# A gated cross-attention kernel with routed experts: attention values for two groups of heads at a time, score maxima moved within the slices, and their rows sent ahead of the second norm

## The chip, the core and the metric

The kernel runs on one core of a Trainium2 chip. The metric is device time in microseconds (us), the median of several runs. The core has five engines that run their own instruction streams and meet only at semaphores: TensorE (PE, matrix products into the accumulator memory PSUM; its weight loads are listed as PEld), VectorE (DVE), ScalarE (ACT), GpSimd (POOL) and SyncE (SP, which here only issues DMAs). Each engine takes its instructions in the order in which the program wrote them.

## What is computed

For 32 sequences of 112 tokens (width 256) and contexts of 375 rows, the reference computes a gated cross-attention with 16 heads of 16 columns, and then a gated mixture of 8 experts, 2 for each token:

```
x = x + tanh(g_xattn) * attention(layernorm(x), ctx, ctx)        # Q, K, V with bias, softmax, Wo, bo
s = softmax(layernorm(x) @ w_router.T);  w, e = top_k(s, 2)
x = x + tanh(g_ffn) * sum_k w_k * expert_{e_k}(layernorm(x))     # silu(t w1) * (t w3), times w2
```

All of it is in float32. The inputs are drawn so that the projections' biases and the router's weights matter.

## The kernel before

The program has two parts. The first, up to 636 us in the trace, is attention with the router, one sequence after the other. The second works through 63 tiles of 128 routed tokens, and the change doesn't touch it.

**The attention loop** is a software pipeline written by hand: on every engine a function `step(i)` runs for i from -3 to 32, and within a step most engines go through 12 slices, k = 0 to 11. Step i works on five sequences at once: the attention proper of b = i, the score maxima of c = i+1, the value projection of s = i+2, norm, query and key projection of a = i+3, and the output projection of e = i-1. The second norm and the router's logits are those of r = i-2. Once in four steps, from i = 6 on, the router's choice for a unit of four sequences is worked out on DVE, in six parts: `route(u, 0..3)` in a step that I call a **routed step** (i = 6, 10, 14, ...), at k = 2, 5, 8 and 11, and `route(u, 4)` and `route(u, 5)` in the step behind it, a **settled step** (i = 7, 11, ...), at k = 2 and 5. The other two of every four are **plain steps**. A short set of statistics for the first norm (L706 and L709, and in the settled ones L556) runs at k = 8 of the routed and the settled steps.

**The pieces on PE**, with their lines:
- `exps(b, k)`, L816: two products with 224 columns in every slice. They recompute the scores of a pair of heads, already less the maxima, and ACT turns them into `probs` (L466). The maxima come in as one more row of `stack`, row 96, for each half of the heads; so k = 0 waits for the rows of the first half and k = 6 for those of the second (`s_nmrow`).
- `maxes(c, t)`, L839: two products with 376 columns, t = 0 to 7, into one pair of PSUM banks. DVE reduces them (L692), and PE may not write the next pair before DVE is done (`s_max`). They stand in slices 0, 1, 3, 4, 6, 7, 9 and 10, directly behind `exps` or `values`.
- `values(b, g)`, L830: 12 products that use 32 columns of the array each, four side by side, for one of four groups of heads. (The trace has two records for each.) They stand one group at a time, in slices 4, 7 and 10, and the fourth in slice 1 of the next step. `probs` has two buffers.
- `key_proj` (L850), `value_proj` (L845), the query projection (L947), the output projection (L986), turns of blocks (L855 for the negated maxima, L921, L859, L967, L939) and the logits (L865).

**The way of the maxima's rows**: DVE reduces (L692), PE turns the 112 x 8 block (L855: half 1 in slice 1, half 0 in slice 5), ACT copies it out (`negmax_out`, L518: half 1 in slice 3, half 0 in slice 6), POOL sends it by two DMAs into row 96 of `stack` (`nm_rows`, L304), and `exps` of slice 6 or of the next step's slice 0 waits until they have landed. POOL runs one list for each step: the second norm of r (L322), `nm_rows` of half 1, the bias for x (L329), a scatter of slots (L310), `nm_rows` of half 0, the four products and the difference that make the split query (L345, L346, L349), and a second scatter.

**Low parts of the keys**: ACT writes the high part of a key block (L492, slices 4 and 9) and DVE the low part (L683, slices 5 and 10), both out of PSUM. Two later pieces of PE reuse these banks and wait for DVE's L683: `value_proj` in slice 6, and the logits in slice 11:

```
if k == 6 and s is not None:
    if a is not None:
        pe.wait_ge(s_klo, DC * a + 1)
    ...
    value_proj(s, 1, BC)
```

In slice 4 DVE takes, ahead of its reduction, a reciprocal and the scaling of the attention output (L670, L673), and in slice 10 the residual of x (L678) ahead of L683.

## Time and profile before

| | us |
|---|---|
| median of 3 runs | 960.62 (959.65 to 963.28) |
| the profiled execution | 959.3 |
| its span, from the first to the last instruction | 957.6 |
| PE busy in the span | 858.1 (90%) |
| DVE, ACT, POOL busy | 492.6, 417.8, 475.0 |
| attention loop from the exps of step 4 to those of step 28 | 446.19 for 24 steps, 18.59 each |

PE's busy time counts overlapping matrix products once, from the start of a group to its modelled end, and the end of one group lies a little behind the start of the next. So the length of a piece in the middle of a stream is read from the chain of waits, where pieces stand end to end, and not from the timeline. TensorE's granted clock is 1.00, its full 2.4 GHz, in all the windows of steps that are spoken of below.

### The profile page before, as it was taken

The page shows a single profiled execution, that of the slowest core. Times are in us where ns is not written, and L with a number is a line of the kernel's source. Part 1 is how long each engine was busy: PE and PEld are TensorE (multiplying, and loading weights), DVE is VectorE, ACT ScalarE, POOL GpSimd, SP SyncE. Part 2 cuts the span into 40 slices and gives each one's busy share as a digit, 9 for nine tenths or more (in the row PEclk, how much of TensorE's full clock was granted, in tenths as well). Part 3 has the DMA queues.
Part 4 walks back from the last instruction along what each step waited for, and adds up shares of the span by engine and source line. Part 5 has one row for each costly group of instructions (what it writes and reads, how often), then busy time and mean ns, then how long its engine had stood idle before and what let it go on. Part 6 is the DMA issues. An engine that isn't in the chain of part 4 may idle for free.

```text
span 957.6 us, 20971 instructions
## 1 busy us (share of the span) xinstructions
PE 858.1 (90%) x7152; PEld 679.4 (71%) x7152; DVE 492.6 (51%) x1155; ACT 417.8 (44%) x1083; POOL 475.0 (50%) x565
## 2 busy tenths in 40 slices
PE   1689999999999999999999999871699999999995
PEld 1467778777878877787778777660477777777774
DVE  1266666765775875775786676646122222222221
ACT  1245555655555565555556555440222222222221
POOL 0654443345455445545544554444366566666553
PEclk9899999999999999999999999995799999999998
DMA  6555665667677666557656654308243443443442
GB/s 174 132 134 138 140 164 137 162 149 179 146 157 163 157 148 154 128 137 163 137 111 141 141 129 112 76 26 191 45 61 62 67 62 62 67 62 62 67 61 27
DMA packets 99246, 110.87 MB, mean 116 GB/s; under 512 B 28668, under 2 KB 80628, under 8 KB 99144
## 3 DMA queue, kind: packets, MB, share of 16 engines
q1 hardware_dynamic: 78936, 91.41, 41.4%
q0 software_dynamic: 18240, 16.83, 11.2%
q10 hardware_dynamic: 1968, 1.31, 0.5%
q8 instruction: 60, 0.98, 0.5%
q14 instruction: 42, 0.34, 0.1%
HBM read 34.11 MB, written 16.15 MB: 52 GB/s over the span
## 4 chain that ended last, share of the span: by engine, by line
PE 76%; DMA 11%; issue 4%; DVE 3%; POOL 3%; SPq 1%; ACTq 1%; ACT 0%; POOLq 0%; DVEq 0%
PE ps L1038 15%; PE ps L839 10%; PE ps L816 9%; PE ps L845 8%; PE ps L1073 8%; PE ps L850 8%; DMA stack<-negmax_t 7%; PE ps L830 7%; PE ps L986 3%; PE ps L1055 2%; DVE negmax L692 2%; POOL stack L304 2%; PE ps L1061 1%; PE ps L939 1%; DMA out_dram<-y,idx 1%
## 5 line engine op out<-in xcount | busy, mean ns | idle before, releaser
L692 DVE TENSOR_REDUCE negmax<-ps 112x2 f32<-112x750 f32 x256 | 240.6, 940 | 179.8 <-PE ps L839 178.3
L466 ACT ACTIVATE probs<-ps 125x448 f32<-125x448 f32 x384 | 208.6, 544 | 246.0 <-PE ps L816 243.5
L816 PE MATMUL ps<-stack 97*125 97x224 f32 x768 | 191.6, 333 | 19.4 <-DMA stack<-negmax_t 19.3
L816 PEld LDWEIGHTS ps<-stack 97*125 97x125 f32 x768 | 129.5, 188 | 47.0 <-DMA stack<-negmax_t 25.6
L839 PE MATMUL ps<-stack 96*112 96x376 f32 x512 | 143.6, 362 | 13.1 <-DVE negmax L692 7.1
L402 POOL DMA_INDIRECT out_dram<-y,idx x63 | 99.9, 1585 | 98.6 <-issue 56.7
L795 DVE TENSOR_TENSOR h<-silu,ps 128x352 f32<-128x352 f32 x63 | 32.8, 521 | 170.9 <-PE ps L1038 170.9
L304 POOL DMA_DIRECT2D stack<-negmax_t x128 | 70.9, 559 | 94.1 <-ACT negmax_t L518 79.4
L322 POOL TENSOR_SCALAR xn<-xa,mv,rstd 112x256 f32<-112x256 f32 x31 | 38.1, 1229 | 159.2 <-DVE rstd L570 159.2
L536 ACT ACTIVATE silu<-ps 128x352 f32<-128x352 f32 x63 | 29.2, 464 | 193.2 <-PE ps L1038 193.2
L845 PE MATMUL ps<-wv_sb,ctx_t 128*125 128x256 f32 x384 | 99.9, 382 | 1.4 <-DVE bo_gated L731 0.9
L830 PE MATMUL ps<-probs,v_sb 125*32 125x112 f32 x3072 | 100.1, 263 | 0.2 <-ACT probs L466 0.2
L839 PEld LDWEIGHTS ps<-stack 96*112 96x112 f32 x512 | 71.8, 177 | 38.2 <-issue 16.6
L310 POOL DMA_INDIRECT slot_table<-pay,slots_i x64 | 62.6, 978 | 67.6 <-PE ps L830 55.7
L850 PE MATMUL ps<-ctx_t,wk_sb 128*128 128x375 f32 x256 | 93.5, 488 | 0.7 <-ACT q_raw L499 0.7
L1073 PE MATMUL ps<-w_sb,h_t 128*128 x378 | 92.1, 380 | 0.7 <-ACT h_t L540 0.7
L1038 PE MATMUL ps<-w_sb,xg_t 128*128 x252 | 86.2, 464 | 0.6 <-ACT xg_t L544 0.6
L1073 PEld LDWEIGHTS ps<-w_sb,h_t 128*128 128x128 f32 x378 | 72.0, 191 | 20.4 <-issue 0.9
L830 PEld LDWEIGHTS ps<-probs,v_sb 125*32 125x32 f32 x3072 | 69.3, 109 | 14.8 <-ACT probs L466 0.3
L393 POOL DMA_INDIRECT xg<-xn_scratch,idx x63 | 61.6, 977 | 29.2 <-issue 18.9
L845 PEld LDWEIGHTS ps<-wv_sb,ctx_t 128*125 128x125 f32 x384 | 68.8, 188 | 8.1 <-issue 1.3
L1038 PEld LDWEIGHTS ps<-w_sb,xg_t 128*128 128x128 f32 x252 | 48.1, 191 | 18.6 <-issue 1.9
(163 smaller groups left out, 1198.5 us busy)
## 6 DMA issues: line engine op xcount, KB each, us to landing
stack<-split SPq DMA_DIRECT2D x256, 150.0 KB
stack<-split SPq DMA_DIRECT2D x128, 94.0 KB
ctx_t<-in_ctx_dram SPq DMA_DIRECT2D x32, 375.0 KB, 4.9
stack<-split SPq DMA_DIRECT2D x128, 56.0 KB
out_dram<-xa SPq DMA_DIRECT2D x32, 112.0 KB, 4.4
xn_scratch<-xn SPq DMA_DIRECT2D x32, 112.0 KB, 4.1
w_sb<-in_L_ffn_w_dram SPq DMA_DIRECT2D x8, 352.0 KB, 4.2
xa<-in_x_dram SPq DMA_DIRECT2D x6, 448.0 KB, 5.9
```

The source lines that it names most:

```text
L304: gp.dma_start(dst[:, :, SKP + SQ * h:SKP + SQ * h + SQ], negmax_t[4 * h:4 * h + 4, half, :].bitcast(f32)).then_inc(s_nmrow[half][c % NSLO ...
L310: gp.indirect_dma_start(table, bass.IndirectOffsetOnAxis(ap=slots_i[:, u % 2, GB * k + j:GB * k + j + 1], axis=0), pay[:, UNITS[u][j], k, ...
L402: gp.indirect_dma_start(out, bass.IndirectOffsetOnAxis(ap=idx[:, t % NI, 0:1], axis=0), y[:, t % NY, :], None, compute_op=ALU.add).then_in ...
L466: act.activation(probs[:, g % 2, ch, :], ps[0:KW, EXPB + k % 2, 0:4 * SQ], ACT.Exp).then_inc(s_exp, 1)
L692: dve.tensor_reduce(negmax[:, half, :, p4], ps[0:SQ, MAXB:MAXB + 2, 0:SK], axis=AX.X, op=ALU.max, negate=True).then_inc(s_max, 1)
L816: last = pe.matmul(ps[0:KW, EXPB + k % 2, QW * m:QW * m + QW], stack[:, b % NSLOT, p, KW * ch:KW * ch + KW], stack[:, b % NSLOT, p, SKP:KQ ...
L830: last = pe.matmul(ps[32 * j:32 * j + 32, PVB, SQ * g:SQ * g + SQ], v_sb[:, b % NSLOT, ch, head, :], probs[:, g % 2, ch, SQ * j:SQ * j + S ...
L839: last = pe.matmul(ps[0:SQ, MAXB + h, 0:SKP], stack[0:ONE_ROW, c % NSLOT, t, SKP + SQ * h:SKP + SQ * h + SQ], stack[0:ONE_ROW, c % NSLOT, ...
L845: last = pe.matmul(ps[0:KW, bank, 0:EMB], ctx_t[:, s % NSLOT, n, KW * ch:KW * ch + KW], wv_sb[:, n, :], start=(n == 0), stop=(n == DC - 1))
L850: last = pe.matmul(ps[:, bank, 0:SK], wk_sb[:, n, P * m:P * m + P], ctx_t[:, a % NSLOT, n, :], start=(n == 0), stop=(n == DC - 1))
L1038: last = pe.matmul(ps[:, bank, 0:F], xg_t[:, t % NS, k, :], w[k][:, bass.ds(e, 1), :].rearrange("p e f -> p (e f)"), start=(k == 0), stop= ...
L1073: last = pe.matmul(ps[:, YB, 0:EMB], h_t[0:n, c, :], w2_sb[0:n, c, bass.ds(e_o, 1), :].rearrange("p e d -> p (e d)"), start=(c == 0), stop ...
```

## The change

Four things are written differently:
- **Values in pairs.** `values(b, 0)` and `values(b, 1)` stand together in slice 7, `values(b, 2)` and `values(b, 3)` together in slice 1 of the next step. For this `probs` gets a third buffer (three scratch tiles of the second part move in memory to make room), and the waits for free buffers and POOL's waits for `s_pv` ahead of its scatters follow.
- **Maxima.** A table `MAX_AT` puts the eight `maxes` into slices 0, 1, 2, 4, 6, 7, 8 and 10, on PE as the last piece of the slice but for those of slice 11, on DVE at the same slices.
- **Rows of the maxima.** ACT's `negmax_out` of half 1 moves from slice 3 to slice 2, ahead of the copy of `pv_t` (L478); POOL's `nm_rows` of half 1 goes in front of the second norm (L322).
- **Half 0.** Its turn on PE moves from slice 5 to slice 6, behind `exps`, and ACT's copy behind `q_raw` (L499).

The core of the diff:

```
+    NPR = 3
-        probs = sb("probs", [KW, 2, KC, 4 * SQ])
+        probs = sb("probs", [KW, NPR, KC, 4 * SQ])
+        MAX_AT = (0, 1, 2, 4, 6, 7, 8, 10)
 # gpsimd
+                if b is not None:
+                    nm_rows(b, 1)
                 if r is not None:
...
-                if b is not None:
-                    nm_rows(b, 1)
...
-                    gp.wait_ge(s_pv, 4 * b + 1)
+                    gp.wait_ge(s_pv, 4 * b)
...
-                    gp.wait_ge(s_pv, 4 * b + 3)
+                    gp.wait_ge(s_pv, 4 * b + 2)
 # scalar
-                            wait(act, s_pv, 4 * b + g - 1)
+                            wait(act, s_pv, 4 * b + g - NPR + 1)
...
+                    if k == 2 and b is not None:
+                        ...
+                        negmax_out(b, 1, BB_)
                     if k == 2 and e is not None:
...
-                    if k == 3 and b is not None:
...
-                        negmax_out(b, 1, BB_)
...
-                    if k == 6 and c is not None:
-                        negmax_out(c, 0, BA)
                     if k == 6 and a is not None:
...
+                    if k == 6 and c is not None:
+                        negmax_out(c, 0, BA)
 # vector
-                    if k % 3 != 2 and c is not None:
-                        t = k // 3 * 2 + k % 3
+                    if k in MAX_AT and c is not None:
+                        t = MAX_AT.index(k)
 # tensor
                     if k == 1 and e is not None:
+                        values(e, 2)
                         values(e, 3)
-                    if k % 3 == 1 and k > 1 and b is not None:
-                        values(b, k // 3 - 1)
-                    if k % 3 != 2 and c is not None:
-                        maxes(c, k // 3 * 2 + k % 3)
+                    if k == 7 and b is not None:
+                        values(b, 0)
+                        values(b, 1)
...
-                    if k == 5 and c is not None:
+                    if k == 6 and c is not None:
...
                         negmax_turn(c, 0, BA)
...
+                    if k in MAX_AT and c is not None:
+                        maxes(c, MAX_AT.index(k))
```

**PE, slices 2 to 6** of one step, before (from `exps` of slice 3, behind the key projection of slice 2). L816 is `exps`, L839 `maxes`, L939 the turn of `pv_t`, L830 `values`, L947 the query projection, L855 the turn of the maxima, L845 a value projection:

```order
L816 MATMUL ps<-stack 125x224 x2
L839 MATMUL ps<-stack 112x376 x2
L939 MATMUL ps<-ident,pv_t 112x128 x4
L816 MATMUL ps<-stack 125x224 x2
L830 MATMUL ps<-probs,v_sb 32x112 x12
L839 MATMUL ps<-stack 112x376 x2
L816 MATMUL ps<-stack 125x224 x2
L947 MATMUL ps<-xn_t,wq_sb 128x112 x4
L855 MATMUL ps<-ident,negmax 8x112
L816 MATMUL ps<-stack 125x224 x2
L839 MATMUL ps<-stack 112x376 x2
L845 MATMUL ps<-wv_sb,ctx_t 125x256 x2
```

The same place now, from the key projection (L852) on. All lines stand two further down up to here: L818 is `exps`, L841 `maxes`, L941, L949, L857 and L847 are the others:

```order
L852 MATMUL ps<-ctx_t,wk_sb 128x375 x2
L841 MATMUL ps<-stack 112x376 x2
L818 MATMUL ps<-stack 125x224 x2
L941 MATMUL ps<-ident,pv_t 112x128 x4
L818 MATMUL ps<-stack 125x224 x2
L841 MATMUL ps<-stack 112x376 x2
L818 MATMUL ps<-stack 125x224 x2
L949 MATMUL ps<-xn_t,wq_sb 128x112 x4
L818 MATMUL ps<-stack 125x224 x2
L857 MATMUL ps<-ident,negmax 8x112
L847 MATMUL ps<-wv_sb,ctx_t 125x256 x2
L841 MATMUL ps<-stack 112x376 x2
```

The group of values has left the place between the two `maxes`, the first `maxes` stands a slice earlier, the turn of the maxima stands behind `exps` of slice 6, and the value projection ahead of the `maxes`.

**DVE, slices 2 to 5 of a routed step**, before: L588 to L593 are `route(u, 0)`, L692 the reduction of the maxima, L670 and L673 the scaling of the output, L683 the low part of the keys:

```order
L588 TENSOR_REDUCE r_max<-lg 112x4
L589 TENSOR_TENSOR r_eq<-lg,r_max 112x32
L590 TENSOR_TENSOR r_eq<-r_eq,first_e 112x32
L591 TENSOR_REDUCE r_col<-r_eq 112x4
L592 TENSOR_TENSOR r_mask<-r_eq,r_col 112x32
L593 SCALAR_TENSOR_TENSOR r_lg<-r_mask,lg 112x32
L692 TENSOR_REDUCE negmax<-ps 112x2
L670 RECIPROCAL rsum<-ps 112x16
L673 TENSOR_TENSOR o_nat<-ps,rsum 112x256
L692 TENSOR_REDUCE negmax<-ps 112x2
L683 SCALAR_TENSOR_TENSOR split<-ps,bk_sb,split 128x375
```

Now (L694 is the reduction, L685 the low part):

```order
L694 TENSOR_REDUCE negmax<-ps 112x2
L590 TENSOR_REDUCE r_max<-lg 112x4
L591 TENSOR_TENSOR r_eq<-lg,r_max 112x32
L592 TENSOR_TENSOR r_eq<-r_eq,first_e 112x32
L593 TENSOR_REDUCE r_col<-r_eq 112x4
L594 TENSOR_TENSOR r_mask<-r_eq,r_col 112x32
L595 SCALAR_TENSOR_TENSOR r_lg<-r_mask,lg 112x32
L672 RECIPROCAL rsum<-ps 112x16
L675 TENSOR_TENSOR o_nat<-ps,rsum 112x256
L694 TENSOR_REDUCE negmax<-ps 112x2
L685 SCALAR_TENSOR_TENSOR split<-ps,bk_sb,split 128x375
```

The reduction of t = 2 stands ahead of the router's part, and the router's part directly ahead of the scaling. In a settled step `route(u, 4)` stands in the same place.

**DVE, slices 7 to 10 of a settled step**, before: L706, L709 and L556 are the statistics, L678 is the residual:

```order
L692 TENSOR_REDUCE negmax<-ps 112x2 x2
L706 BN_STATS st<-xa 112x6 x2
L709 BN_AGGR mv<-st 112x2 x2
L556 TENSOR_SCALAR half<-mv 112x4
L692 TENSOR_REDUCE negmax<-ps 112x2
L678 SCALAR_TENSOR_TENSOR xa<-ps,tanh_g,xa 112x256
L683 SCALAR_TENSOR_TENSOR split<-ps,bk_sb,split 128x375
```

Now:

```order
L694 TENSOR_REDUCE negmax<-ps 112x2 x3
L708 BN_STATS st<-xa 112x6 x2
L711 BN_AGGR mv<-st 112x2 x2
L558 TENSOR_SCALAR half<-mv 112x4
L680 SCALAR_TENSOR_TENSOR xa<-ps,tanh_g,xa 112x256
L685 SCALAR_TENSOR_TENSOR split<-ps,bk_sb,split 128x375
```

The third reduction has moved ahead of the statistics, which now stand directly ahead of the residual and the low part.

## Rows read from the trace of the kernel before

**Rows 1.** Windows: length, busy time by engine, clock, DMA share; 24 steps, then steps 16 to 19.

```profile
129.34:575.53 446.19, 431.80 (x4462) 354.56 (x4462) 309.57 (x718) 256.13 (x666) 217.97 (x304) 1.00 0.65 147
351.77:370.05 18.28, 17.89 (x187) 14.69 (x186) 11.45 (x25) 10.84 (x29) 9.42 (x14) 1.00 0.67 162
370.05:388.66 18.61, 17.87 (x187) 14.67 (x186) 11.04 (x22) 10.58 (x27) 9.44 (x14) 1.00 0.60 134
388.66:407.76 19.10, 18.36 (x194) 15.10 (x194) 15.35 (x44) 10.70 (x28) 9.60 (x14) 1.00 0.60 132
407.76:425.88 18.12, 17.86 (x187) 14.66 (x186) 13.54 (x34) 10.58 (x27) 9.28 (x13) 1.00 0.58 137
```

**Rows 2.** Waits in the same 24 steps: total us, times, longest.

```profile
PE ps L816 <- DMA stack<-negmax_t: 12.8, 24, 1.1
```

**Rows 3.** Chain of waits in step 19, end to end: start, us, piece.

```profile
409.63 0.71 PE ps L830 x24
410.35 0.53 PE ps L839 x2
...
411.39 1.27 PE ps L850 x4
...
412.88 0.35 PE ps L839 x2
413.23 0.44 PE ps L939 x4
...
416.74 0.48 PE ps L816 x2
```

**Rows 4.** Timeline of PE: start, length, line; prologue, step 19, step 30.

```profile
32.37 1.13 PE L845 MATMUL ps<-wv_sb,ctx_t 128*125 128x256 f32 x4 [0.43 <-DVE split L683]
...
415.17 1.05 PE L947 MATMUL ps<-xn_t,wq_sb 128*128 128x112 f32 x8
416.24 0.26 PE L855 MATMUL ps<-ident,negmax 112*8 112x112 f32 x1
...
615.15 0.60 PE L839 MATMUL ps<-stack 96*112 96x376 f32 x2 [0.49 <-DVE negmax L692]
...
627.68 0.78 PE L830 MATMUL ps<-probs,v_sb 125*32 125x112 f32 x24
628.39 0.26 PE L855 MATMUL ps<-ident,negmax 112*8 112x112 f32 x1
```

**Rows 5.** Timeline of ACT in step 19, slices 2 and 3.

```profile
411.43 0.54 ACT L466 ACTIVATE probs<-ps 125x448 f32<-125x448 f32 x1 [0.57 <-PE ps L816]
...
413.35 0.24 ACT L518 ACTIVATE negmax_t<-ps 8x112 fp32r<-8x112 f32 x1
```

**Rows 6.** Timeline of DVE: routed step 18, settled step 19, and step 30.

```profile
393.12 0.18 DVE L588 TENSOR_REDUCE r_max<-lg 112x4 f32<-112x32 f32 x1
...
394.46 0.94 DVE L692 TENSOR_REDUCE negmax<-ps 112x2 f32<-112x750 f32 x1
...
402.18 0.74 DVE L706 BATCH_NORM_STATS2 st<-xa 112x6 f32<-112x256 f32 x2
...
403.12 0.16 DVE L604 TENSOR_TENSOR r_exp<-lg,r_max 112x32 f32<-112x32 f32 x1
...
403.50 0.93 DVE L612 TENSOR_TENSOR cum<-cum,r_new 112x8 bf16<-112x8 bf16 x1
...
412.22 0.18 DVE L622 TENSOR_REDUCE r_inv<-r_exp 112x4 f32<-112x32 f32 x1
...
413.43 0.94 DVE L692 TENSOR_REDUCE negmax<-ps 112x2 f32<-112x750 f32 x1
414.28 0.25 DVE L670 RECIPROCAL rsum<-ps 112x16 f32<-112x16 f32 x1
414.56 0.42 DVE L673 TENSOR_TENSOR o_nat<-ps,rsum 112x256 f32<-112x256 f32 x1
...
416.01 0.60 DVE L683 SCALAR_TENSOR_TENSOR split<-ps,bk_sb,split 128x375 fp32r<-128x375 f32 x1
```

**Rows 7.** Issue to landing of the maxima's row DMAs, 200 to 580 us.

```profile
DMA to landing us min/median/max: 1.8/4.3/5.6
```

**Rows 8.** Timeline of POOL in routed step 18: the second norm, the last product of the query.

```profile
393.45 1.24 POOL L322 TENSOR_SCALAR xn<-xa,mv,rstd 112x256 f32<-112x256 f32 x1 [4.64 <-DVE rstd L570]
...
403.28 1.14 POOL L349 TENSOR_TENSOR split<-q_msk,split 128x448 fp32r<-128x448 f32 x1
```

More of the change, by code:

```diff
@@ L111, in flamingo @@
         idx = sb("idx", [P, NI, 2], i32)
+        e_cmp, e_mul, e_mul2 = (sb(n, [1, TW, NE]) for n in ("e_cmp", "e_mul", "e_mul2"))
         xg, xg_t = sb("xg", [P, NXG, EMB]), sb("xg_t", [P, NS, DC, P])
```

9 lines of the change are left out of this document (4 added, 5 removed).

## The prediction

> **What bounds the kernel now.** I read the windows of the attention loop first. In 24 steps PE is busy 431.8 of 446.2 us, DVE 309.6, ACT 256.1 and POOL 218.0 [rows 1]. So PE's list sets the pace, 18.59 us a step, and the other engines count only where PE waits for them. The table of waits names one place with a wait in every one of the 24 steps: `exps` of slice 6, for the rows of the maxima of half 1, 12.8 us in all, 0.53 a step and 1.1 at most [rows 2]. The change can gain in two ways: by a shorter list on PE, and by taking this wait away. I then put together the new order from the lengths in the chain and looked for what is late next.
>
> I count from **T, the end of `exps` in slice 2**. End to end, undisturbed pieces take: key projection 1.27, `maxes` 0.35, turn of `pv_t` 0.44 [rows 3], `exps` 0.22 (224 columns where `maxes` has 376; between 409.42 and 409.63 of the chain, estimated from 0.35 x 224/376), query projection 0.88 (1.05 less an overlap of 0.17) [rows 4], value projection 0.87 (the 1.13 of a lone one less 0.26, by which such a piece overlaps the one before).
>
> **The shorter list.** One group of values takes 0.71, the `maxes` behind it 0.53 instead of 0.35 [rows 3]. So leaving the 32-column pieces costs 0.18. Entering costs some 0.14: the 24 records stand for six rounds of 112 columns x four side by side, 0.095 each by the tempo of the other pieces, 0.57 in all, and 0.71 less that is 0.14. That is an estimate; its bounds are 0 and 0.2. Four groups apart have four entries and four exits, two pairs have two of each: 2 x 0.14 + 2 x 0.18 = 0.64 saved. In slice 1 the piece behind the values is now the small turn L855, which in step 30 ends 0.19 behind them (628.65 against 628.46) where 0.10 is its own length [rows 4]: 0.09 more. **0.73 a step.** That the `maxes` stand behind a large piece I cost at nothing: 0.35 behind `exps` is 2 x 376 columns at 2.4 GHz plus 0.03, so there is nothing left to hide. (Below nothing isn't excluded: 0.03 x 4.)
>
> **The wait for the rows.** Step 19 takes 18.12 [rows 1]. In it `exps` of slice 6 ends 0.72 behind the end of L855 (417.22 against 416.50) where 0.22 would do, and L855 ends 0.28 behind the query projection, since it waits for DVE, where 0.10 would do [rows 3, 4]. So a step without waits is 18.12 - 0.50 - 0.18 = 17.44, and in the new order 17.44 - 0.73 = **16.71**.
> The rows need 3.15 us from the end of L518 to the start of `exps` in step 19 (413.59 to 416.74) [rows 3, 5], with an idle time of 0.24; with the mean idle of 0.53 that is 3.44, with the longest 4.0. Now L518 stands in slice 2, behind its exponential, which starts at T + 0.04; the next ACT instruction starts 0.44 later [rows 5], so L518 ends at T + 0.72. POOL is free then: the norm L322 (1.24) [rows 8], which ended 0.2 behind L518 before, inside the 0.63 from L518 to POOL's DMA, now comes after and is wanted only in slice 9. Rows land so that `exps` starts at T + 4.16 (3.87 to 4.7) and ends at T + 4.64.
>
> **What is late next: DVE.** Only `exps` and the turn of `pv_t` are left between `maxes` 2 and 3, and they share PSUM banks.
> - PE ends `maxes` 2 at T + 1.62. DVE reduces from 1.65 to 2.59 (0.94) [rows 6]. PE starts `maxes` 3 at 2.65, and alone it takes 0.60 [rows 4]: 3.25, where 2.85 would be undisturbed.
> - DVE reduces t = 3 from 3.28; L683 starts 0.86 behind that, at 4.14, and takes 0.60 [rows 6]: 4.74. The value projection of slice 6 waits for it: start 4.80, and 1.13 for a lone one [rows 4] is T + 5.93.
> - Undisturbed it would end at 1.62 + 0.22 + 0.44 + 0.22 + 0.35 + 0.22 + 0.88 + 0.22 + 0.10 + 0.87 = 5.14; with the rows alone at 4.64 + 0.97 = 5.61.
> So a **plain step** waits 0.79, of which the rows add 0.03 in their latest cases: 16.71 + 0.82 = 17.53, against 18.28 and 18.61 before.
>
> **Routed and settled steps.** Before, the router's part ran on DVE in the shadow of the key projection, ahead of t = 2. Now it runs between t = 2 and the scaling. It takes 1.34 in a routed step (393.12 to 394.46) and 1.21 in a settled one (412.22 to 413.43) [rows 6].
> - Routed: free at 1.65 + 0.86 = 2.51, router's part to 3.85, L670 and L673 another 0.28 + 0.37 to 4.50, t = 3, L683 from 5.36 to 5.96, value projection from 6.02 to 7.15: it waits 2.01.
> - Settled: the same with 1.21: 7.02, 1.88.
> In slices 8 to 10 it is alike. From the end E of the value projection of slice 6, PE ends `maxes` 6 at E + 4.40 (`maxes` 0.35, `exps` 0.22, two groups 1.29, turn 0.35, `maxes` 0.35, `exps` 0.22, key projection 1.27, `maxes` 0.35). DVE is free at 5.29, then come the statistics (0.94) and in the routed step four short instructions (0.38 and a last one of 0.15) [rows 6], or one more in the settled step (0.22), then L678 (0.39) and L683 (0.60): ready at 7.81 or 7.50. The logits would start at E + 7.16 (another 0.22 + 0.19 + 0.87 + 0.22 + 0.35 + 0.22 + 0.87, less the overlap of two pieces, 0.16 to 0.18). With 0.08 for a lone start they wait 0.7 or 0.4. Plain steps have nothing there.
> Routed: 16.71 + 2.01 + 0.7 + 0.48 for the ranks (PE busy 18.36 against 17.88) [rows 1] = **19.90**, against 19.10 before. Settled: 16.71 + 1.88 + 0.4 = **18.99**, against 18.12 in step 19.
>
> **The sum.** Four steps: 17.53 + 17.58 (one of the plain ones has three more short DVE instructions) + 19.90 + 18.99 = 74.0, against 4 x 18.59 = 74.36: -0.36, and for the 24 steps -2.2. Steps 1 to 3 and 28 have no router's part: 4 x -0.9 = -3.6. In the last steps no projections stand between the `maxes`, and PE would wait for DVE there (615.15, 0.60 after 0.49 idle [rows 4], is this case); the last two groups of values end 0.58 later than one did: +1, bounds -1 and +4. Together **-4.8**: 959.3 becomes 954.5. The median of the runs lies 1.3 above the profiled execution, so 955.8; I say **956**. The second part isn't touched.
>
> **Rivals.**
> - *The router's work stays hidden* (936). If DVE had slack that I don't see, so that routed and settled steps waited like plain ones, four steps would be 70.6, -3.7, and the 24 steps -22. Against it: DVE takes its list in order, and 1.65 + 0.94 is fixed by PE's `maxes` 2. Chance 0.13.
> - *The rows land late* (970, slower). They are now sent 1.5 us earlier, deeper in SP's 16 copies into `stack`. From DMA issue to landing they take 1.8 to 5.6, median 4.3, over both halves [rows 7]; half 1 in step 19 took about 2.5 of the 3.15. Above 3.76 from L518 each 0.1 costs 0.1 in the 16 steps without router's part, and up to the 4.9 or so at which it shows in the others too. At 4.65 that is 0.9 x 16 = +14. It decides from 4.4 on (+10, above the time before). Chance 0.14.
> - *DVE and POOL block each other* (961). L612 took 0.93 [rows 6], and it ends where POOL's L349 ends, at 404.42 [rows 8], while its like take 0.15 to 0.2. The norm L322 now runs from T + 2.5 to T + 3.7, beside the router's part. Had that to wait, it would cost 0.8 in six steps, +5. Against it: in step 18 the six instructions ran beside L322 (393.45 to 394.69) [rows 8] and took no more than 1.34. Chance 0.05. The Trainium skill ("SBUF — State Buffer", Who interferes with whom) says that a DVE instruction with two SBUF inputs contends with a GpSimd instruction that reads SBUF, and that the one issued second fully blocks. By that rule the time would be this rival's; the trace agrees at L612 and does not at L322.
> - *The pairs don't shorten the list* (965). If an entry costs nothing and the group's length is its own, 0.28 x 31 = 9 of the gain is missing. Chance 0.05, inside "same".
>
> **Chances.** My sum 0.63, with a range of its own of 950 to 962, since 0.1 a step is 3 us. About 0.5% (4.8 us) is what a measurement of this kernel can tell from no change: below 955.8 is faster, above 965.4 slower. Faster 0.30 + 0.13 = 0.43, same 0.33 + 0.05 + 0.05 = 0.43, slower 0.14. The range 941 to 966 leaves out most of the first two rivals.
>
> **What would show it.** In the profile after: the wait of PE for the row DMAs gone or under 0.2 a step; in its place waits of L841 (`maxes` 3) and of L847 for DVE, L847's 0.4 to 0.8 in plain steps and nearly 2 in routed ones; `values` as 48 records in about 1.29; steps of 17.5, 17.6, 19.9 and 19.0. It is wrong if routed steps are shorter than 19, if L818 still waits over half a microsecond for its rows, or if the pairs take over 1.4.

## The result and the profile after

| | before | changed |
|---|---|---|
| median of 4 runs each | 961.24 us (959.65 to 963.28) | 1007.0 us (998.6 to 1012.07) |
| profiled execution, span | 959.3, 957.6 | 1012.07, 1010.3 |
| granted clock of TensorE, mean over the span | 0.971 | 0.930 |

The ratio is 1.0466 (95% interval 1.0378 to 1.0555): slower by 45.8 us, where I had forecast 956 and a range of 941 to 966.

Windows of the changed kernel: first the stretch of time of [rows 1], then the same 24 steps (4 to 27), then steps 16 to 19. Columns as in [rows 1].

```profile
129.34:575.53 446.19, 412.46 (x4076) 344.60 (x4076) 281.15 (x649) 229.02 (x609) 197.95 (x278) 0.94 0.59 136
129.37:619.68 490.31, 451.49 (x4462) 377.25 (x4462) 311.08 (x720) 251.27 (x666) 217.31 (x304) 0.94 0.58 134
374.46:395.30 20.84, 19.08 (x187) 16.00 (x186) 12.07 (x27) 10.62 (x29) 9.38 (x13) 0.92 0.60 142
395.30:413.36 18.06, 17.45 (x187) 14.71 (x186) 11.02 (x22) 10.32 (x27) 9.43 (x13) 1.00 0.65 138
413.36:435.57 22.21, 19.95 (x194) 16.51 (x194) 14.82 (x41) 10.43 (x28) 9.39 (x13) 0.92 0.50 112
435.57:458.32 22.75, 20.57 (x186) 17.09 (x186) 14.14 (x35) 10.46 (x27) 9.41 (x13) 0.85 0.48 111
```

The 24 steps take 490.3 where they took 446.2: +44.1 of the 52.7 us between the two spans. The same 4462 records keep PE busy 19.7 us longer, and it sits idle 24.4 us longer (38.8 against 14.4). Both come at the same steps: the six routed ones cost 23.8 more together, the six settled ones 17.3, the plain ones that follow a settled one 4.6, and the other plain ones are 1.6 faster. (The remaining 8.6 of the 52.7 stand behind step 28, where the clock is at 0.50 for longer too: for 10.2 in step 30, and for 54.6 instead of 41.0 where the second part begins.) The clock was 1.00 in the whole stretch before [rows 1]; now it is 0.85 to 0.92 in three of these four steps. Before, the page's row of the granted clock had no 8 inside the loop; the changed kernel's has five behind the start:

```profile
PEclk9899999899899899989989999975599999999998
```

The waits of PE in these 24 steps (total us, times, longest), where [rows 2] had the row DMAs alone with 12.8:

```profile
PE ps L857 <- DVE negmax L694: 12.5, 10, 1.9
PE ps L818 <- DMA stack<-negmax_t: 12.2, 14, 1.5
PE ps L847 <- ACT xn_t L512: 7.7, 24, 0.3
PE ps L841 <- DVE negmax L694: 4.4, 24, 0.2
PE ps L847 <- DVE split L685: 1.2, 7, 0.2
```

The wait for the rows has not gone, it stands in 14 steps instead of 24. PE's long wait for DVE stands one piece ahead of where I looked for it: at the turn L857, which needs the reduction that DVE does just before L685; the value projection L847 behind it waits only 1.2 in all. Two new waits stand in every step: L841 for DVE, as forecast, and the value projection of slice 11 for ACT's copy of the turned second norm (L512), which I had not foreseen. Now routed step 10, PE, DVE and POOL around slice 6 (start, length, line; in brackets the idle time ahead):

```profile
257.03 0.48 PE L818 MATMUL ps<-stack 97*125 97x224 f32 x2 [1.04 <-DMA stack<-negmax_t]
258.07 0.34 PE L857 MATMUL ps<-ident,negmax 112*8 112x112 f32 x1 [0.57 <-DVE negmax L694]
258.49 2.07 PE L847 MATMUL ps<-wv_sb,ctx_t 128*125 128x256 f32 x4
```

```profile
253.29 0.94 DVE L694 TENSOR_REDUCE negmax<-ps 112x2 f32<-112x750 f32 x1 [0.43 <-PE ps L841]
254.15 0.17 DVE L590 TENSOR_REDUCE r_max<-lg 112x4 f32<-112x32 f32 x1
...
255.20 0.90 DVE L594 TENSOR_TENSOR r_mask<-r_eq,r_col 112x32 f32<-112x32 f32 x1
256.14 0.19 DVE L595 SCALAR_TENSOR_TENSOR r_lg<-r_mask,lg 112x32 f32<-112x32 f32 x1
256.36 0.26 DVE L672 RECIPROCAL rsum<-ps 112x16 f32<-112x16 f32 x1
```

```profile
254.12 1.23 POOL L326 TENSOR_SCALAR xn<-xa,mv,rstd 112x256 f32<-112x256 f32 x1
255.33 0.72 POOL L331 TENSOR_TENSOR xa<-xa,bo_gated 112x256 f32<-112x256 f32 x1
```

A settled step has the same at another instruction, here L628 of step 11, beside a bias that runs from 278.88 to 279.60:

```profile
278.48 1.16 DVE L628 SCALAR_TENSOR_TENSOR pay<-r_exp,tanh_g,r_inv 112x4 f32<-112x4 f32 x1
```

Three things are to be seen. The router's part takes 254.15 to 256.36, 2.21 instead of the 1.34 of [rows 6]: its L594, whose like take 0.19, takes 0.90 and ends at 256.10, with POOL's addition of the bias (256.05). PE is idle twice in a row. And behind that, from 257.98 on, the granted clock is 0.50 (1.2 GHz) for 6.8 us, and the value projection takes 2.07 instead of 1.13. Twelve such stretches of 3.4 or 6.8 us stand in the 24 steps, each behind idle time of PE of 1.2 to 2.0 us. PE is busy for 57.1 us of their 58.0, so at full clock they would be some 28.5 shorter (an estimate): that, and not 19.7, is the clock's loss in these steps. The two differ because the list itself got shorter, to 17.45 us of busy time in a plain step at full clock where it was 17.88. The four runs of the changed kernel order themselves by it: clocks 0.930, 0.934, 0.941 and 0.947 go with 1012.1, 1011.7, 1002.3 and 998.6.

### The profile page after: what moved, and what is told of

Read it like the earlier page. It is cut to its first block, busy times and chain, and to the rows that moved or that the text cites. A ratio compares the mean times of both kernels' runs of the same rounds, so it can differ in the third digit from the quotient of the medians.

```text
span 1010.3 us, 20970 instructions
## 1 busy us (share of the span) xinstructions
PE 886.7 (88%) x7152; PEld 712.1 (70%) x7152; DVE 493.7 (49%) x1155; ACT 412.7 (41%) x1083; POOL 474.8 (47%) x565
## 4 chain that ended last, share of the span: by engine, by line
PE 74%; DVE 9%; DMA 7%; issue 5%; ACT 2%; SPq 1%; POOL 1%; ACTq 1%; POOLq 0%; DVEq 0%
PE ps L1042 15%; PE ps L847 10%; PE ps L832 9%; PE ps L1077 8%; PE ps L841 8%; PE ps L852 7%; PE ps L818 6%; DVE negmax L694 4%; DMA stack<-negmax_t 4%; PE ps L988 3%; PE ps L1059 2%; PE ps L1065 1%; PE ps L969 1%; DMA out_dram<-y,idx 1%; PE ps L867 1%
## 5 line engine op out<-in xcount | busy, mean ns | idle before, releaser
L694 DVE TENSOR_REDUCE negmax<-ps 112x2 f32<-112x750 f32 x256 | 240.5, 939 | 221.9 <-PE ps L841 220.3
L841 PE MATMUL ps<-stack 96*112 96x376 f32 x512 | 175.8, 426 | 17.4 <-DVE negmax L694 14.2
L818 PE MATMUL ps<-stack 97*125 97x224 f32 x768 | 163.4, 297 | 16.1 <-DMA stack<-negmax_t 16.1
L818 PEld LDWEIGHTS ps<-stack 97*125 97x125 f32 x768 | 137.6, 195 | 22.7 <-DMA stack<-negmax_t 19.5
L847 PE MATMUL ps<-wv_sb,ctx_t 128*125 128x256 f32 x384 | 113.3, 421 | 12.2 <-ACT xn_t L512 9.0
L841 PEld LDWEIGHTS ps<-stack 96*112 96x112 f32 x512 | 85.1, 188 | 48.9 <-DVE negmax L694 22.8
L852 PE MATMUL ps<-ctx_t,wk_sb 128*128 128x375 f32 x256 | 95.7, 497 | 0.7 <-ACT q_raw L499 0.7
L847 PEld LDWEIGHTS ps<-wv_sb,ctx_t 128*125 128x125 f32 x384 | 69.5, 201 | 29.5 <-ACT xn_t L512 14.1
L832 PEld LDWEIGHTS ps<-probs,v_sb 125*32 125x32 f32 x3072 | 82.3, 121 | 8.3 <-issue 2.7
L852 PEld LDWEIGHTS ps<-ctx_t,wk_sb 128*128 128x128 f32 x256 | 45.6, 197 | 18.1 <-issue 1.7
```

The costliest lines, as they stand in the source:

```text
L694: dve.tensor_reduce(negmax[:, half, :, p4], ps[0:SQ, MAXB:MAXB + 2, 0:SK], axis=AX.X, op=ALU.max, negate=True).then_inc(s_max, 1)
L818: last = pe.matmul(ps[0:KW, EXPB + k % 2, QW * m:QW * m + QW], stack[:, b % NSLOT, p, KW * ch:KW * ch + KW], stack[:, b % NSLOT, p, SKP:KQ ...
L832: last = pe.matmul(ps[32 * j:32 * j + 32, PVB, SQ * g:SQ * g + SQ], v_sb[:, b % NSLOT, ch, head, :], probs[:, (4 * b + g) % NPR, ch, SQ * ...
L841: last = pe.matmul(ps[0:SQ, MAXB + h, 0:SKP], stack[0:ONE_ROW, c % NSLOT, t, SKP + SQ * h:SKP + SQ * h + SQ], stack[0:ONE_ROW, c % NSLOT, ...
L847: last = pe.matmul(ps[0:KW, bank, 0:EMB], ctx_t[:, s % NSLOT, n, KW * ch:KW * ch + KW], wv_sb[:, n, :], start=(n == 0), stop=(n == DC - 1))
L852: last = pe.matmul(ps[:, bank, 0:SK], wk_sb[:, n, P * m:P * m + P], ctx_t[:, a % NSLOT, n, :], start=(n == 0), stop=(n == DC - 1))
```

## Experiments: the parts of the change apart

Three kernels take one part each, on top of the kernel before. They are compared with runs of the kernel before of their own (median 963.64).

**The rows alone.** ACT's L518 in slice 2 instead of 3, POOL's row DMAs ahead of the second norm:

```diff
-                if k == 3 and b is not None:    # ACT: negmax_out(b, 1, BB_)
+                if k == 2 and b is not None:
+            if b is not None:                   # POOL, ahead of the second norm
+                nm_rows(b, 1)
```

> The kernel before with the rows of half 1 sent earlier alone (ACT's copy in slice 2, POOL's DMAs ahead of the second norm). Theory A: nothing else moves, DVE keeps its shadows, so the wait of 0.53 us a step at exps of slice 6 goes, with the 0.25 of a lone start: 0.5 to 0.75 x 31 = 15 to 23 us less, 938 to 946, clock 0.97. Rival C (the rows land later when they are sent earlier, among more of SP's copies): the wait stays over 0.3 us a step, 950 or more.

Measured: 943.9 (942.2 to 947.5), 0.979 [0.974, 0.984]. Again in five rounds:

> The kernel before with the rows' move alone, once more and in more rounds, since it is the version that would be kept: 0.979 of the kernel before (0.974 to 0.984), as in the first run.

942.8 (940.9 to 947.7), 0.981 [0.978, 0.985]. The windows of steps 16 to 19 of the first of the two:

```profile
343.14:361.38 18.24, 17.88 (x187) 14.67 (x186) 11.44 (x25) 10.84 (x29) 9.39 (x14) 1.00 0.67 162
361.38:379.11 17.73, 17.71 (x186) 14.65 (x186) 11.05 (x22) 10.60 (x27) 9.39 (x14) 1.00 0.61 141
379.11:397.35 18.24, 18.22 (x194) 15.09 (x194) 15.27 (x44) 10.72 (x28) 9.58 (x14) 1.00 0.62 138
397.35:415.08 17.73, 17.70 (x186) 14.66 (x186) 13.21 (x34) 10.60 (x27) 9.22 (x13) 1.00 0.59 140
```

Every step is shorter than in [rows 1], and in three of the four PE is idle for 0.03 or less: the wait for the rows was all that these steps had to lose. It is faster than both kernels, and as theory A said.

**The pairs alone**, values of two groups in slices 1 and 7, with the third buffer and the waits that belong to it:

```diff
-                    if k % 3 == 1 and k > 1 and b is not None:
-                        values(b, k // 3 - 1)
+                    if k == 7 and b is not None:
+                        values(b, 0)
+                        values(b, 1)
```

> The kernel before with the values in pairs alone (three probs buffers and the waits that follow; maxima, rows and router's parts where they were). Theory A (waits make the loss, and the clock follows them): PE's list is 0.7 us a step shorter, but the group of values that filled slice 4 is gone while the rows of the maxima still come from slice 3, so the wait of slice 6 grows by about as much as the list shrinks: 18.4 to 18.8 us a step, 957 to 968, and the granted clock stays at 1.00 in the loop unless a single wait gets past 1.5 us. Rival B (the long stretch of 32-column pieces itself makes the clock fall): half-clock stretches inside the loop, mean clock at or under 0.94, over 985.

Measured: 1004.9 (1001.1 to 1011.3), 1.042 [1.036, 1.049]. Its waits from 128 to 600 us (its lines are one on from before's: L817 `exps`, L840 `maxes`, L846 the value projection):

```profile
PE ps L817 <- DMA stack<-negmax_t: 21.4, 23, 2.0
PE ps L840 <- DVE negmax L693: 14.5, 28, 1.2
PE ps L846 <- ACT xn_t L511: 4.7, 16, 0.3
```

The group of values in slice 4 was not only work: it stood between two `maxes` and gave DVE 0.71 to reduce, and it gave the row DMAs the same time. With it gone PE waits for both, and plain steps take 19.1 to 19.8 where the clock stays up. Neither expectation came: the time is 37 above theory A's, and the granted clock (0.952 to 0.960) is above rival B's, with half-clock stretches in four of the 24 steps. That the long piece of 32 columns lowers the clock by itself is ruled out further down: two versions with the same pairs (973.1 and 949.7) keep 1.00 in all 24 steps.

**The table alone**, `maxes` in slices 0, 1, 2, 4, 6, 7, 8, 10 and behind the large piece:

```diff
-                    if k % 3 != 2 and c is not None:
-                        maxes(c, k // 3 * 2 + k % 3)
+                    if k in MAX_AT and c is not None:   # behind the slice's large piece
+                        maxes(c, MAX_AT.index(k))
```

> The kernel before with the new places of the maxima alone (slices 0, 1, 2, 4, 6, 7, 8, 10, last in the slice; turn of half 0 in slice 6), values one group at a time, rows from slice 3. Theory A: here DVE's router parts and statistics already fall out of the shadow of the key projections, so routed and settled steps get waits of 1 to 2 us for DVE's low part of the keys, and the granted clock falls behind some of them: 970 to 1000, mean clock under 0.965. Rival B (pairs are to blame): as before within 1%, clock 0.97.

Measured: 982.1 (977.6 to 986.6), 1.017 [1.011, 1.023]; the one wait is L817 for the rows, 30.2 us in 25 places. The time is in the range of theory A, but the place was not: no wait for DVE shows. With the rows still late, their wait covers DVE's work; the next run, with early rows, has that wait for DVE.

**Two parts together.** The rows and the table, with the values one group at a time:

> The kernel before with two of the three parts of the change: the rows' DMAs early, and the maxima in slices 0, 1, 2, 4, 6, 7, 8, 10 with the small turns that go with them; the values stay one group at a time, in slices 1, 4, 7, 10. It fills slice 4 with values again, 0.71 us of work between the maxima of t = 2 and t = 3. Theory A (the pair takes the filler away, and with the filler back DVE has the time for t = 2 and the router's part): routed and settled steps lose 0.7 of their waits, the clock stays up, plain steps about 17.7 to 17.9: 948 to 958. Theory B (the table alone brings the waits, since L857 and L847 hang on the same reductions of DVE with or without the pair): 965 to 985, with waits of L841 or L847 for DVE in routed steps and half-clock windows behind them.

Measured: 965.5 (964.0 to 968.6), 1.004 [1.001, 1.007]. Plain steps take 17.7 and 18.0 to 18.6, routed ones 19.76 where the clock stays up, settled ones 19.04. Theory B: L856 (the turn of the maxima) waits for DVE 12 times, 10.9 us, and half-clock stretches stand in two routed steps, so the filler in slice 4 does not give DVE the time for its router's part. A part of it is not the table's order alone: in the six settled steps L627, the router's instruction that is L628 in the changed kernel, takes 1.16 beside POOL's bias, as there.

The rows and the pairs, with the maxima in the old slices:

> The kernel before with the other two parts: the rows' DMAs early, and the values of two groups at a time in slices 1 and 7; the maxima stay in slices 0, 1, 3, 4, 6, 7, 9, 10. The pairs alone gave 1004.9, with PE's waits for the rows (29.0 us in 31 places) and for DVE's maxima (24.6 in 43). Theory A (of those only the rows' wait goes; between the maxima of t = 2 and 3, in slices 3 and 4, there stands now only exps and a turn, and PE waits for DVE in every step, 0.5 to 0.6): plain steps 17.6 to 18.2, routed 19 to 20, 955 to 975. Theory B (the early rows take away the last long wait, and the shorter list shows): plain steps 17.0 to 17.3 and a time of 925 to 940, below the 943.9 of the rows alone.

Measured: 973.1 (968.3 to 979.5), 1.011 [1.007, 1.014]. Theory A by the time, with plain steps longer than it said, 18.3 to 19.6; L840 waits for DVE in 31 places, 15.1 us, and the clock stays at 1.00 in all 24 steps. So beside the early rows (-18 to -20 us) the table costs 22 and the pairs 30, each without the other, and the two together 64.

## Experiments: what the new order runs into

These start from the changed kernel (1007.0) and move one small thing of another engine. Their runs of the kernel before have medians of 959.9 to 963.6.

**Router's parts on DVE** in slices 5, 6, 7 instead of 2, 5, 8 (settled: 5, 6 instead of 2, 5), the statistics in slice 0 instead of 8:

```diff
-                    if routed is not None and k in (2, 5, 8):
+                    if routed is not None and k in (5, 6, 7):
-                    if settled is not None and k in (2, 5):
+                    if settled is not None and k in (5, 6):
```

> The changed kernel with DVE's list alone altered: router's parts 0, 1, 2 of a routed step behind the low part of the keys and behind the reductions of slices 6 and 7 (slices 5, 6, 7 instead of 2, 5, 8), parts 4 and 5 of a settled step in slices 5 and 6 instead of 2 and 5, the statistics of the first norm in slice 0 instead of 8. Theory A: routed and settled steps wait like plain ones, the clock stays at 1.00 through the loop, all steps take 18.1 to 18.6 us (plain ones were 18.05 to 18.9 in the changed kernel): 945 to 958, clock 0.97. Rival B (pairs or the new list as such lower the clock): half-clock stretches stay, over 985.

Measured: 968.6 (965.1 to 975.5), 1.004 [1.001, 1.007]: 38 us off, theory A in its direction, but 11 to 24 short. Settled steps fall to 18.05, routed ones only to 20.0 to 20.8 where the clock stays up (the last to 18.9), and the half clock is left in two stretches of 3.4. The router's second part now meets POOL's row DMAs and its split of the query (L347 from 251.27 to 251.84):

```profile
250.83 0.54 DVE L598 TENSOR_TENSOR r_eq<-r_lg,r_max 112x32 f32<-112x32 f32 x1
251.41 0.50 DVE L599 TENSOR_TENSOR r_eq<-r_eq,first_e 112x32 f32<-112x32 f32 x1
```

**POOL's bias later.** Only L331 moves, behind the scatter of the slots, which stands ahead of the row DMAs of half 0. (This expectation and four later ones say behind the split of the query; in the kernels that ran it stands ahead of that split, as here.)

```diff
-                if c is not None:   # POOL, behind the second norm
-                    gp.tensor_tensor(xrow(c), xrow(c), bo_gated[:, :], ALU.add)
+                if c is not None:   # behind place(u, j, 0), ahead of nm_rows(c, 0)
+                    gp.tensor_tensor(xrow(c), xrow(c), bo_gated[:, :], ALU.add)
```

> The changed kernel with POOL's addition of the bias (L331, 0.72 us) moved behind POOL's split of the query, so that behind the norm L326 POOL reads no SBUF row beside the router's part on DVE. Theory A (DVE and POOL block each other: the router's part took 2.21 us instead of 1.34 in the changed kernel, its instruction of L594 0.90 and ending with L331): L594 falls to about 0.2, the routed step's wait of L847 falls by 0.7, six steps, 4 us and, since the wait before the clock's fall gets shorter, perhaps some half-clock time too: 0.988 to 0.998 of the changed kernel, 995 to 1003 beside its 1007. Theory B (the clock and the order decide, the port is a side matter): the time stays within 3 us of the changed kernel's, or the blocking moves to L326 or to the next POOL instruction.

Measured: 975.4 (972.5 to 980.0), 1.016 [1.011, 1.021], against 1.047: **one instruction of 0.72 us on an engine that is busy half the time was worth 32 us**, between two and three times the most that theory A allowed (12). DVE and POOL in step 10:

```profile
251.32 0.20 DVE L594 TENSOR_TENSOR r_mask<-r_eq,r_col 112x32 f32<-112x32 f32 x1
251.55 0.19 DVE L595 SCALAR_TENSOR_TENSOR r_lg<-r_mask,lg 112x32 f32<-112x32 f32 x1
251.77 0.26 DVE L672 RECIPROCAL rsum<-ps 112x16 f32<-112x16 f32 x1
```

```profile
251.66 1.03 POOL L312 DMA_INDIRECT slot_table<-pay,slots_i  x1 [0.21 <-issue]
252.72 0.74 POOL L336 TENSOR_TENSOR xa<-xa,bo_gated 112x256 f32<-112x256 f32 x1
```

The router's part takes 250.27 to 251.77, 1.50. The same execution holds its own counter-test: up to step 7 no scatter stands in POOL's list, so there the bias still follows the norm directly, and L594 takes 0.90 in step 6 and L628 1.15 in step 7; from step 10 on they take 0.19 to 0.20 and 0.23, though the norm still runs beside them. Undisturbed steps of this kernel are 19.93 routed and 18.94 settled: my 19.90 and 18.99. The blocking itself is 0.7 in a routed step and, by L628 (1.16 on the average of five in the changed kernel, 0.38 of six here), 0.8 in a settled one, some 9 us of DVE's time. The larger part is the clock, at 0.50 in two stretches of 3.4 in steps 4 to 27 instead of twelve: of the 30.0 us between the two traces in these steps 23.9 are busy time of the same records (451.5 and 427.6), and 6.1 are idle time, nearly all of it at the turn L857 (12.5 and 6.3).

**The copy earlier.** ACT's L512 in slice 9 instead of 10 (`if k == 10 and r is not None` becomes `k == 9`):

> The changed kernel with ACT's copy of the turned second norm (L512) one slice earlier in ACT's list, in slice 9 instead of 10. In the changed kernel PE's value projection of slice 11 waits for it in every step (end to end 1.45 where 0.87 would do, +0.58). Theory A (the wait is one of order on ACT and can be taken away): that piece falls to 0.87 to 0.95 and the step by 0.5, 28 x 0.5 = 14 us: 990 to 996. Rival B (PE comes by 0.5 earlier at the next wait, the maxima of slices 1 and 4 or the rows, and waits there instead): the wait for L512 goes from the table, those for DVE and the row DMAs grow, and the time stays above 1002. Rival C: ACT's exponential of slice 9 is late by the copy and delays the values: the wait of PE for ACT's exponentials appears.

Measured: 993.4 (982.0 to 995.2), 1.032 [1.024, 1.039]: theory A, 13.6 off. Steps without half clock and without rows' wait go from 18.06 to 17.48. But the routed and settled steps hardly gain by it where the clock stays up (19.93 with L512 in either place, 18.94 and 18.77, in the versions with the bias moved), and of the 20.0 us between the two traces in steps 4 to 27 15.7 are busy time of the same records, most of it the clock's, which is at 0.50 for 30.7 us instead of 58.0. So that 13.6 lies near 28 x 0.5 is in part luck.

**The bias and the copy.** This is my forecast's kernel with its two overlooked costs taken away:

> The changed kernel with the two small moves that each took time off alone, together: POOL's bias (L331) behind the split of the query, and ACT's copy L512 in slice 9. The router's parts stay where the change left them. This is the forecast's own model with the two things that it missed taken away. Theory A (the forecast missed the blocking of DVE by POOL's bias, with the clock's fall behind it, and the wait for the copy, and nothing else): plain steps 17.5, routed 19.4 to 19.9, settled 18.4 to 18.9, no half clock in the loop but a window or two, and a time of 956 to 963. Theory B (something further is missing, such as the rows' landing in every step): plain steps stay above 17.8 and the time above 966.

Measured: 969.8 (960.5 to 973.9), 1.008 [1.004, 1.011]; its profiled execution was the fastest of its six, 960.5 with a clock of 0.967 (three of the others 971.8 to 973.9 at 0.949 to 0.951). First its 24 steps, then steps 16 to 19, in that:

```profile
128.46:578.03 449.57, 423.12 (x4463) 355.92 (x4462) 302.15 (x719) 253.09 (x666) 218.15 (x304) 1.00 0.62 146
355.31:373.67 18.36, 17.18 (x186) 14.69 (x186) 11.67 (x26) 10.73 (x29) 9.43 (x13) 1.00 0.68 161
373.67:391.15 17.48, 17.32 (x187) 14.70 (x186) 10.99 (x23) 10.42 (x27) 9.44 (x13) 1.00 0.62 143
391.15:411.08 19.93, 18.10 (x195) 15.03 (x194) 14.59 (x43) 10.54 (x28) 9.43 (x13) 1.00 0.55 125
411.08:429.84 18.76, 17.75 (x186) 14.65 (x186) 13.09 (x35) 10.43 (x27) 9.44 (x13) 1.00 0.58 135
```

By the median this is theory B (above 966); the steps of the fastest execution are those of theory A but for the first, which stays at 18.36: theory B's rows, in that kind of step. The half clock stands once in the 24 steps, in step 6, where the bias still follows the norm. What the slower executions lose, beyond their lower clock, no trace shows.

**Router's parts and copy**, and **all three moves**:

> The changed kernel with both: the router's parts on DVE moved as in the run with 968.6 (slices 5 to 7 instead of 2, 5, 8; the statistics in slice 0), and ACT's copy L512 in slice 9. Theory A (both waits are taken away and nothing takes their place): 968.6 - 28 x 0.5 = 952 to 957, steps of about 17.5 in plain and settled and 19.5 in routed ones, near what the forecast's own sum had. Rival B (the rows' landing or DVE's maxima are next, since PE comes earlier to them): 962 to 968. Both expect the granted clock at 1.00 in nearly all of the loop.

> The changed kernel with all three: router's parts on DVE in slices 5 to 7 and the statistics in slice 0, ACT's copy in slice 9, POOL's bias behind the split of the query. Without the bias move the time was 949.7. Theory A (the bias still blocks or delays something there, as the first norm's rows and the scatter before it): routed steps fall from 19.6 towards 19.0 and the time to 943 to 949. Theory B (in slices 5 to 7 the router's part runs beside POOL's split of the query whatever the bias does, and moved behind that split the bias now stands beside it too): no change or up to 4 slower, 949 to 954. By neither does it come below the kernel before with the rows' move alone (943.9) by much.

Measured: 949.7 (944.9 to 957.2), 0.989 [0.985, 0.992], and 954.4 (949.2 to 958.1), 0.990 [0.986, 0.993]. The first is below both theories, the second at theory B's upper end. Plain steps with the rows in time and settled ones take 17.48. With the router's parts elsewhere the bias in its old place blocks nothing, and in its new one it does: L592 takes 0.66 beside it in five routed steps, L627 0.66 in five settled ones. So moving it too brings nothing, and may cost a little. The best that the whole change reached is 11 us faster than before; its rows alone bring 18.

## Experiments: does the clock follow the wait

**Before, with a longer wait.** In the kernel before, the scaling L683 of slice 5 is done five times in the steps with a router's part:

```diff
+                        for _ in range(EXTRA if k == 5 and routed is not None else 0):   # EXTRA = 4
+                            link(dve.scalar_tensor_tensor(out=split[...], ...))
```

> The kernel before, with one thing added: in every fourth step (those with the router's part) DVE's scaling of the key in slice 5 (L683 of before, 0.60 us) is done five times instead of once, writing the same values, so that PE's value projection of slice 6 waits for DVE once, for some 2 us (4 x 0.60 = 2.4, less what slack there is). Nothing else moves; the values' pieces, the rows and the maxima stand as before. Theory A (the granted clock falls behind idle time of PE, whatever makes it idle): half-clock windows of 3.4 to 6.8 us stand behind these waits in the six routed steps, as they did in the changed kernel behind its routed steps; a routed step costs 2.0 to 2.4 for the wait and another 1.7 to 3.4 for the clock, in all 4 to 6 us; seven such steps make +28 to +42, a time of 988 to 1005. Theory B (the clock falls for something else in the changed kernel, such as the 48 narrow value records in a row with a wait on either side): the granted clock of the loop stays at 1.00 and the cost is the waits alone, 7 x 2.0 to 2.4 = +14 to +17, a time of 975 to 980.

Measured: 980.4 (977.4 to 981.9), 1.020 [1.017, 1.023]: at the upper end of theory B's range by the time, but with theory A's half clock in half of the places. In step 6 (L821 `exps`, L850 the value projection):

```profile
174.58 0.48 PE L821 MATMUL ps<-stack 97*125 97x224 f32 x2 [0.82 <-DMA stack<-negmax_t]
...
176.50 1.28 PE L850 MATMUL ps<-wv_sb,ctx_t 128*125 128x256 f32 x4 [1.09 <-DVE split L688]
177.28 0.89 PE L821 MATMUL ps<-stack 97*125 97x224 f32 x2
```

From 177.35 on the clock is 0.50 for 3.4 us. That happens in three of the six routed steps between 4 and 27 (21.9 to 22.2); the other three have the same idle time (0.60 and 1.33 in step 10) and keep 1.00 (21.2 to 21.6). So the clock falls in the old order too, behind a wait put there on purpose, and not behind every one. What decides between them stays open. The kernel before has such a case as well: its step 23 holds 1.8 us of idle time at a clock of 1.00.

**DVE longer with the bias moved.** In the version with the bias moved (975.4), L594 is done four times:

```diff
+                    for _ in range(4):
                         link(dve.tensor_tensor(r_mask[:, 0, 0:n, :], eq, over_e(col), ALU.is_equal))
```

> The changed kernel with POOL's bias behind the split of the query (the version with 975.4 and half-clock windows in only two steps), and in it one instruction of the router's part on DVE (r_mask<-r_eq,r_col, 0.20 with its link 0.22) done four times instead of once, writing the same values: 3 x 0.22 = 0.66 us more in the routed steps, about what the blocking by the bias cost there (2.21 against 1.34); the settled steps are untouched. Theory A (the bias did its harm by the length of PE's wait, and the clock falls behind the longer wait): routed steps 20.6 plus 1.7 to 3.4 each, half-clock windows back in four to seven of the routed steps, time 983 to 995. Theory B (the blocking works in some other way, or the clock hangs on the settled steps too): routed steps 20.6, no more half-clock windows than without, time 978 to 981.

Measured: 995.4 (993.1 to 1000.5), 1.036 [1.031, 1.041]: theory A, just above its range. The clock falls to 0.50 in all six routed steps, which take 23.1 to 24.5, and once more in a settled one. But the addition was not as clean as meant. DVE and POOL in step 10:

```profile
255.74 1.47 DVE L595 TENSOR_TENSOR r_mask<-r_eq,r_col 112x32 f32<-112x32 f32 x4
257.25 0.70 DVE L596 SCALAR_TENSOR_TENSOR r_lg<-r_mask,lg 112x32 f32<-112x32 f32 x1
```

```profile
256.09 1.04 POOL L312 DMA_INDIRECT slot_table<-pay,slots_i  x1 [0.21 <-issue]
257.15 0.74 POOL L336 TENSOR_TENSOR xa<-xa,bo_gated 112x256 f32<-112x256 f32 x1
```

0.66 us of DVE's own work pushed the next one (L596) beside the bias, where it took 0.70 and ended at 257.95 with the bias (257.89); and one of the four repeats took 0.80 beside the scatter. The wait grew by some 1.8, not 0.66. So the longer wait brings the half clock back, but its length is again in part POOL's blocking, and the run doesn't tell the two apart. It does show that the new place of the bias is good only for DVE parts that end before it.

**Rows and bias, in the old order:** the kernel with the rows alone, and in it the bias behind the scatter.

> The kernel before with the rows' move alone (943.9) and POOL's bias behind the split of the query. Theory A (with the old order the router's part on DVE stands in the shadow of the key projection, and what the bias blocks there is hidden): no change, 942 to 947. Theory B (the bias, which waits for the norm, delays the scatter and with it the later rows of SP and POOL in routed steps, where the rows' wait is still 0.5): routed steps 18.2 instead of 18.2 to 18.9, 938 to 942.

Measured: 944.1 (941.9 to 946.0), 0.980 [0.977, 0.984]: theory A. In the version with the rows alone no DVE instruction is held by the bias; here, in its new place, it holds the router's L596 (0.63 instead of 0.19) in five steps and L630 (0.78 instead of 0.18) in five, and the time stays the same. The old order hides such blocking.

## Why the prediction was wrong

- **The shorter list (0.73 a step): right.** The 48 records take 1.29, the small turn behind them 0.19. A plain step with nothing in its way takes 17.48 (forecast 17.53), once the copy is out of it.
- **Maxima behind a large piece, nothing: right.** In step 17 of the version with bias and copy moved they take 0.34 to 0.36 end to end behind the projections.
- **`maxes` 3 waits for DVE: right.** It does so in every step (24 waits, 4.4), and ends some 0.4 late, as forecast.
- **Routed and settled steps, 19.90 and 18.99: right without the blocking and at full clock,** where they are 19.93 and 18.8 to 18.9. In the routed ones the rows come so late that `exps` of slice 6 waits for them 0.7 to 1.4, and DVE's L685 ends as late all the same (401.34 in step 18, T + 6.06 where I had 5.96): that the late rows cost nothing there is partly luck. In the kernel itself these steps are 22.2 to 23.6 and mostly 21.4 to 22.8.
- **The rival "DVE and POOL block each other": the mechanism that came, given 0.05 and a price of 5 us, where moving the bias brought 32.** I looked for a collision with the norm (L322 before), found that step 18 had none [rows 6, 8], and stopped. What blocks is the next instruction on POOL, the bias. Before, the router's part ended at 394.46, ahead of it; after the change DVE's part is later by one reduction, POOL's norm and bias follow the early row DMAs, and they meet. The blocking is visible before too, in L612 with 0.93 [rows 6], but in a place where DVE had slack; now L614 takes 0.17, and L594 and L628 take 0.90 and 1.16. The Trainium skill ("SBUF — State Buffer", Who interferes with whom) has DVE instructions with two SBUF inputs contend with GpSimd instructions that read SBUF. The trace agrees for POOL's TENSOR_TENSOR. For its TENSOR_SCALAR (the norm) it hardly does: where only the norm ran beside them, these DVE instructions took 0.36 at most, mostly 0.19, and L628 0.23 in the version with the bias moved, with the norm in the same place beside it.
- **The clock at 1.00 throughout: the step that failed.** The forecast puts it at nothing, and its only ground, which it doesn't even name, is that the trace of before has 1.00 in the loop [rows 1]. PE's waits before were 0.5 in each step; I forecast waits of 2.0 and 1.9 us in two of every four steps and priced them at their length. Lengthened by the blocking, they had the clock fall behind them in twelve stretches in 24 steps, against two once the bias is out of the way. That costs some 28.5 us (the estimate above), the largest part of what the 24 steps lose. In the two traces with the bias moved, waits of the size that I had forecast mostly leave the clock up; so the blocking, given 0.05, and the clock, put at nothing, failed together. Without the clock's loss the profiled execution would still be at some 984, outside my range.
- **Not foreseen: the copy L512.** The value projection of slice 11 needs it, ACT does it in slice 10, and with 0.7 us less work on PE between the two it comes 0.32 late, 0.58 end to end with what a lone start costs. 28 steps of that would be 16; 13.6 were measured, but not all of them are this wait (see there). I had followed DVE's list and the rows past the moved pieces, but not ACT's.
- **The rows: late in half of the steps, which was one of my signs of being wrong.** PE still waits for them 14 times in 24 steps, 0.9 on average. L520 ends at T + 0.72, as forecast. In steps 16 and 18 of the version with bias and copy moved, `exps` of slice 6 starts 4.6 and 4.8 after that, where I had taken 3.44 and said that it shows from 3.76 on. In routed steps DVE's wait covers it; in the first plain step of four it costs 0.8 (18.36 against 17.58). POOL issues there 0.6 to 0.9 behind L520's end, so 3.7 to 4.2 are the DMA's, where step 17 gets by with under 3.0 (issue 379.13, `exps` 382.10; it takes 0.48, the length of a lone start, so even there the rows were only just in time). Why it takes longer in two kinds of step stays open.

Put together, from the profiled executions: forecast 954.5; the rows in six steps +5; 960.5 measured with bias and copy moved; the copy, the blocking and the clock +51.6 to 1012.1. These are the fastest of six runs and the slowest of four, so the near agreement at 960 is partly luck, and 51.6 is too much: it is 37 in the medians. Moved one at a time, the copy is worth 14 and the bias 32 in the medians, 37 together, so they share a part of the clock's loss. The median of the version with both is 969.8, 14 above the forecast; its runs differ by 13, and but for two neighbours they again order themselves by the clock.

## What to carry to other kernels

Where PE's list sets the pace, work that is taken out from between two waits may have been cover and is then not saved: price a gap by who needs the time in it, on all other engines, and walk every queue (here ACT's copy and POOL's next instruction) past the moved pieces. A forecast that puts waits of one to two us on PE in a loop that has had the full clock needs a term for the clock, with a range, since it fell behind some of such waits and not behind others. And try the parts of a change alone: here the smallest, a row DMA issued one slice earlier, was worth 18 us, and the two that shorten or even out PE's list cost more than that.

## What the hardware showed

- The granted clock fell to 0.50 behind idle stretches of PE of 1.2 to 2.0 us in one or more pieces (1.21 in step 16, 1.04 and 0.57 in step 10), with PE 88% busy or more in the steps around, and stayed there for 3.4 or 6.8 us; in the version with the copy earlier it fell behind 0.98 in step 12. Behind like waits it sometimes did not fall (1.62 in step 27 of the changed kernel).
- DVE instructions of 0.19 us with two SBUF inputs stood for up to 0.9 us beside a POOL TENSOR_TENSOR of 0.72 that began while they ran (L594 from 255.20, the bias from 255.33), and ended with it. L628, otherwise 0.23, took 1.16 and ended with the bias too, though by the trace the bias began only 0.40 after it; recorded starts on POOL are rough. One of 0.19 took 0.79 or 0.80 beside POOL's indirect DMA in five of six steps (the version with L594 done four times), and ended just behind it.
